# Decoder layer on one core: routing mixture on the anchors alone, adapter factor in two halves, FFN products redistributed

## The chip, the cores and the metric

The kernel runs on one core of a Trainium2 chip. The metric is the device time of one execution in microseconds. A core has TensorE (PE: matmuls, with weight loads shown apart as PEld), VectorE (DVE), ScalarE (ACT), GpSimd (POOL) and a queue engine SP that issues DMAs; each runs its own list of instructions in order and they meet only by semaphores.

## The reference, cut to what matters

One decoder layer over x of 2 sequences x 256 tokens x 512 (512 tokens in all): a Mamba-like mixer (128 heads of 64 channels), a product with a quantised context, and an FFN with a routed low-rank adapter. Only the last part is touched:

```
H = x @ W.T + b                      # 512 x 512
z = x @ A                            # rank 32
anchors = arange(1, T, 2)            # every second token, 128 of a sequence's 256
logits  = 0.5*H[anchors,:8]/max|.| + 0.5*(z[anchors] @ LiMEs.T)/max|.|
probs   = softmax(logits); weights = normalised(probs * sigmoid((probs - 2nd best)/0.5))
p_mix   = repeat(weights, 2 tokens) @ LiMEs          # 512 x 32, equal for both tokens of a pair
out     = x_before + H + ((z * p_mix) @ Bmat) * 0.5
```

## The kernel before, in words

All 512 tokens lie in one piece. Tiles of the layer's end are four token tiles t = 0..3 of 128 tokens; tiles 0 and 1 are the first sequence, 2 and 3 the second. Some 770 us go to the mixer: 64 slots (pairs of heads) in a software pipeline in which TensorE projects, scans and projects back. The change touches nothing there. Then comes a hand-written tail, in which the order of each engine's instructions is the order of the code.

The tail's last stage, the FFN, is where the change lies. `ffn(t, passes)` (L1284) issues up to three passes of the FFN product of token tile t into its own PSUM bank `work[t]` (`ps_h`, `ps_z`, `ps_y`, `ps_t` for t = 0..3): upper x upper, upper x lower, lower x upper part of numbers split in two, each pass 4 matmuls of 128x512 at line L1243. Between these passes stand TensorE's small steps for the routing, each waiting for VectorE or ScalarE:

- L1316 and L1320: turn the anchors' H and multiply the anchors' z by LiMEs.
- L1325 and L1328: the two maxima turned and spread to all partitions.
- L1334: when VectorE has the weights (`MIX_WT`, its last step is L1042), two transposes bring them to [8 experts, 256 anchors] in PSUM. ScalarE copies them to `wT` (L658).
- L1338: one plain fp32 matmul (recorded as two) makes the mixture `p_mix`, with `wT` read twice per anchor by a broadcast pattern, so that 512 columns come out.

From there the adapter's factor is made: VectorE multiplies z, the constant and the mixture to `zp` (L1048, 32x512); ScalarE rounds it to the upper part in `zst` (L661) and once more into the next 32 rows (L662); VectorE subtracts the upper part from `zp` for the lower part (L1052). `zst` (96 rows, held in tile `y_hi`) is the stationary operand of four closing matmuls, one for each token tile (L1346), which add the adapter to the four FFN banks (`d_mm`). VectorE adds bank, residual and row sum into `acc` (L1057), tile by tile, and SP stores each tile (L271).

Semaphores: `mix_dve` counts VectorE's routing steps, `mix_act` ScalarE's, `mix_pe` TensorE's; the constants `MIX_WT` and `MIX_ZP` are counts of `mix_dve`. Before the change TensorE waits once, ahead of all four closing matmuls:

```
eng.wait_ge(mix_dve, MIX_ZP + 1)
eng.wait_ge(mix_act, 5)
```

Of the kernel before, what the change touches and what calls it, by code (L numbers as in the profile page):

```python
# [6 lines left out]
B, S = 2, 256  # L7
T = B * S
P = 128
# [14 lines left out]
EXPERTS, RANK = 8, 32  # L24
# [5 lines left out]
OUT_SCALE = 16.0 / RANK  # L30
# [12 lines left out]
def build(nc, x_d, ctx_d, wdt_d, dtpar_d, normw_d, wmain_d, wbc_d, quant_d, wffn_d, ffnb_d,  # L43
# [5 lines left out]
    with ExitStack() as ctx:  # L49
# [67 lines left out]
        limes = sb("limes", [EXPERTS, RANK])  # L117
# [310 lines left out]
        def _(eng):  # L428
# [230 lines left out]

            eng.wait_ge(mix_dve, MIX_ZP)  # L660
            eng.activation(zst[0:RANK, :], zp, ACT.Copy).then_inc(mix_act, 1)  # L661
            eng.activation(zst[RANK:2 * RANK, :], zp, ACT.Copy).then_inc(mix_act, 1)  # L662


        @block.vector
        def _(eng):
# [311 lines left out]
            def mix(ins):  # L978
                n_mix[0] += 1
                ins.then_inc(mix_dve, 1)  # L980
# [42 lines left out]
            for b in range(B):  # L1023
# [23 lines left out]
            eng.wait_ge(mix_pe, 5)  # L1047
            mix(eng.scalar_tensor_tensor(out=zp, in0=zh[0:RANK, :], scalar=OUT_SCALE, in1=ps_out[0:RANK, 0, :],  # L1048
                                         op0=ALU.mult, op1=ALU.mult))
            assert n_mix[0] == MIX_ZP  # L1050
            eng.wait_ge(mix_act, 4)
            mix(eng.tensor_tensor(zst[2 * RANK:3 * RANK, :], zp, zst[0:RANK, :].bitcast(f32), ALU.subtract))  # L1052
            for t in range(TT):
# [8 lines left out]
        def _(eng):  # L1062
# [221 lines left out]
            def ffn(t, passes=(0, 1, 2)):  # L1284

                eng.wait_ge(x_add, t + 1)
                eng.wait_ge(ffn_low, 1)
                eng.wait_ge(low_wbc, GROUPS + 1)
                products(work[t][:], lambda k: wffn(k, True), lambda k: wffn(k, False), t, passes)
# [39 lines left out]
            ffn(1, (2,))  # L1329
            ffn(2, (0, 1))  # L1330

            eng.wait_ge(mix_dve, MIX_WT)
            for b in range(B):
                done = tr(ps_out[0:EXPERTS, 1, b * P:(b + 1) * P], ffn_small[:, 7, b, :])  # L1334
            done.then_inc(mix_pe, 1)
            ffn(2, (2,))
            eng.wait_ge(mix_act, 3)
            mm(ps_out[0:RANK, 0, :], limes[:], wT.unsqueeze(2).broadcast_to([EXPERTS, T // 2, 2]), start=True,  # L1338
               stop=True).then_inc(mix_pe, 1)
            ffn(3)  # L1340
            eng.wait_ge(mix_dve, MIX_ZP + 1)
            eng.wait_ge(mix_act, 5)
            eng.wait_ge(bstlo_done, 1)
            eng.wait_ge(bst_done, 2)
            for t in range(TT):
                mm(work[t][:], zst[:, t * P:(t + 1) * P], bst, start=False, stop=True,  # L1346
                   skip_group_check=True).then_inc(d_mm, 1)
# [93 lines left out]
```

## Time and profile before

| | us |
|---|---|
| median of 3 runs (lowest, highest) | 816.22 (814.41, 816.71) |
| the profiled execution's own time | 814.25 |
| its span in the trace | 812.4 |
| TensorE busy (matmul) | 787.0 |
| VectorE / ScalarE / GpSimd busy | 615.7 / 603.5 / 624.1 |
| granted TensorE clock, mean | 0.996 |

The span runs from the first to the last recorded event. Times in the trace are from the span's start. A matmul's duration includes its way through the array, so that consecutive ones overlap: what a matmul costs a stream is the distance between starts. In the grouped lines the columns are the line, engine, operation, output<-inputs, shapes and count, then busy us and mean ns of one, then the idle time before it and what ended that.

### The profile page before, as it was taken

How to read it: one execution, taken by the hardware profiler on the slowest of the kernel's cores; microseconds unless marked ns; L12 is line 12 of the kernel's file. 1: busy time of each engine (PE TensorE's matmuls, PEld its weight loads, DVE VectorE, ACT ScalarE, POOL GpSimd, SP SyncE). 2: the span in 40 equal slices, each digit the busy share in tenths (PEclk: the TensorE clock that was granted, in tenths of full speed). 3: DMA queues.
4: the chain of work that ended last, by engine and by line, in shares of the span. 5: the costliest groups of instructions: out<-in, count | busy, mean ns of one | idle time of the engine just before them, and what ended most of it. 6: DMA issues, size and time to landing. Idle time of an engine off the chain costs nothing.

```text
span 812.4 us, 13296 instructions
## 1 busy us (share of the span) xinstructions
PE 787.0 (97%) x4322; PEld 607.8 (75%) x4322; DVE 615.7 (76%) x752; ACT 603.5 (74%) x1052; POOL 624.1 (77%) x552
## 2 busy tenths in 40 slices
PE   8798999999999999999999999999999999999897
PEld 7576777777777777777777777777777777777664
DVE  6889978786776867786776867776786867798864
ACT  5788777877788776877688886878688876888442
POOL 6689985799578985799578985799578986798231
PEclk9999999999999999999999999999999999999999
DMA  8452425333243324334233424333233424340001
GB/s 332 146 142 86 130 67 177 122 118 130 92 134 123 129 65 158 127 129 129 91 129 129 129 65 156 129 129 129 91 129 129 129 66 157 130 126 30 4 2 52
DMA packets 48812, 94.93 MB, mean 117 GB/s; under 512 B 3952, under 2 KB 36848, under 8 KB 48784
## 3 DMA queue, kind: packets, MB, share of 16 engines
q1 hardware_dynamic: 48496, 94.06, 35.0%
q10 hardware_dynamic: 288, 0.52, 0.2%
q8 instruction: 15, 0.25, 0.1%
q14 instruction: 13, 0.11, 0.0%
HBM read 93.26 MB, written 1.31 MB: 116 GB/s over the span
## 4 chain that ended last, share of the span: by engine, by line
PE 58%; DVE 21%; ACT 11%; issue 8%; POOL 1%; DMA 0%; ACTq 0%; DVEq 0%
PE ps_z L1093 17%; PE ps_out L1196 14%; PE ps_h L1093 12%; PE ps_y L1183 6%; DVE conv L728 5%; DVE conv_bc L728 4%; ACT decay L531 4%; DVE yg L852 2%; PE ps_t L1066 2%; ACT L531 2%; DVE v L846 2%; ACT conv L477 2%; DVE y_lo L858 2%; DVE decay L792 1%; ACT conv_bc L461 1%
## 5 line engine op out<-in xcount | busy, mean ns | idle before, releaser
L728 DVE SCALAR_TENSOR_TENSOR conv<-ps_h,w_raw,conv 128x510 f32<-128x510 f32 (+2 forms) x192 | 143.2, 746 | 94.5 <-ACT conv L477 90.0
L531 ACT ACTIVATE decay<-csx,cs_own 128x256 f32<-128x256 f32 (+1 forms) x512 | 184.4, 443 | 1.0
L297 POOL TENSOR_TENSOR win_lo<-w_raw,win_hi 128x1024 fp32r<-128x1024 f32 x64 | 153.4, 2397 | 0.5 <-DMA csx<-cs_rows 0.5
L399 POOL TENSOR_TENSOR sqacc<-sqacc,sq 128x512 f32<-128x512 f32 x47 | 70.3, 1496 | 94.1 <-ACT sq L567 94.1
L792 DVE TENSOR_TENSOR decay<-decay,cbm 128x1536 f32<-128x1536 f32 x64 | 126.0, 1968 | 2.4 <-ACT decay L531 2.4
L539 ACT ACTIVATE hidT<-conv 128x512 f32<-128x512 f32 x64 | 40.5, 634 | 94.8 <-DVE conv L728 94.8
L1183 PE MATMUL ps_y<-decay,hid_dt 128*64 128x256 f32 (+1 forms) x1024 | 97.5, 333 | 9.4 <-DVE hid_dt L835 9.4
L337 POOL TENSOR_SCALAR_AFFINE_SELECT csx<-csx 128x512 f32<-128x512 f32 x128 | 105.8, 851 | 0.2 <-DMA csx<-cs_rows 0.2
L1183 PEld LDWEIGHTS ps_y<-decay,hid_dt 128*64 128x64 f32 x1024 | 63.4, 136 | 51.9 <-issue 17.3
L1196 PE MATMUL ps_out<-wout_hi,y_lo 128*128 128x512 f32 x252 | 99.9, 397 | 0.0
L1196 PE MATMUL ps_out<-wout_lo,y_hi 128*128 128x512 f32 x252 | 99.5, 395 | 0.0
L1196 PE MATMUL ps_out<-wout_hi,y_hi 128*128 128x512 f32 x252 | 99.4, 395 | 0.0
L302 POOL TENSOR_TENSOR wout_lo<-w_raw,wout_hi 128x512 fp32r<-128x512 f32 x64 | 94.1, 1470 | 0.1
L858 DVE SCALAR_TENSOR_TENSOR y_lo<-yg,w_raw,y_hi 128x512 fp32r<-128x512 f32 x64 | 92.7, 1448 | 1.6 <-ACT y_hi L561 1.6
L531 ACT ACT_TABLE_LOAD x63 | 80.8, 1283 | 1.2
L1093 PE MATMUL ps_z<-hT_hi,win_hi 128*128 128x512 f32 x256 | 77.1, 423 | 0.5 <-DVE conv_bc L728 0.3
L1093 PE MATMUL ps_h<-hT_hi,win_hi 128*128 128x512 f32 x256 | 73.5, 408 | 0.0
L1093 PE MATMUL ps_z<-hT_lo,win_hi 128*128 128x512 f32 x256 | 70.6, 397 | 0.0
L1093 PE MATMUL ps_h<-hT_lo,win_hi 128*128 128x512 f32 x256 | 70.2, 396 | 0.0
L1093 PE MATMUL ps_z<-hT_hi,win_lo 128*128 128x512 f32 x256 | 69.9, 394 | 0.0
L1093 PE MATMUL ps_h<-hT_hi,win_lo 128*128 128x512 f32 x256 | 69.3, 392 | 0.0
L288 POOL TENSOR_SCALAR win_hi<-w_raw 128x1024 fp32r<-128x1024 f32 x63 | 65.7, 1043 | 0.0
(316 smaller groups left out, 1483.0 us busy)
## 6 DMA issues: line engine op xcount, KB each, us to landing
w_raw<-in_wmain SPq DMA_DIRECT2D x64, 772.0 KB, 4.3
csx<-cs_rows SPq DMA_DIRECT2D x128, 256.0 KB, 3.5
bc_raw<-in_wbc SPq DMA_DIRECT2D x8, 517.0 KB, 3.5
ctx_raw<-in_ctx SPq DMA_DIRECT2D x1, 2048.0 KB, 16.4
bc_raw<-in_wffn SPq DMA_DIRECT2D x2, 512.0 KB, 4.0
out_x<-acc SPq DMA_DIRECT2D x4, 256.0 KB, 2.1
acc<-in_x ACTq DMA_DIRECT2D x2, 256.0 KB, 3.7
acc<-in_x SPq DMA_DIRECT2D x2, 256.0 KB, 3.5
```

Of the source, the lines that this page charges most:

```text
L288: eng.tensor_scalar(win_hi[:, r2, :], w_raw[:, r4, 0:W_IN], 1.0, 0.0, ALU.mult, ALU.add).then_inc(hi_win, 1)
L297: eng.tensor_tensor(win_lo[:, r2, :], w_raw[:, r4, 0:W_IN], win_hi[:, r2, :].bitcast(f32), ALU.subtract).then_inc(low_win, 1)
L302: eng.tensor_tensor(wout_lo[:, r4, :], w_raw[:, r4, W_IN:W_ALL], wout_hi[:, r4, :].bitcast(f32), ALU.subtract).then_inc(low_wout, 1)
L337: eng.affine_select(out=blocks[:, :, to:to + P], in_=blocks[:, :, at:at + P], compare_op=ALU.is_ge, fill=never, base=0, pattern=[[0, 2 * B ...
L399: eng.tensor_tensor(sqacc[:], sqacc[:], sq[:, (k - 1) % 2, :], ALU.add).then_inc(pool_sq, 1)
L531: done = eng.activation(decay[:, r2, b, h, lo:lo + n], csx[:, r2, b, h, lo:lo + n], ACT.Exp, bias=cs_own[:, r2, t, h:h + 1])
L728: eng.scalar_tensor_tensor(out=out_b[:, :, back:], in0=src_b[:, :, 0:S - back], scalar=w[:, TAPS - 1 - back:TAPS - back], in1=out_b[:, :, ...
L792: eng.tensor_tensor(decay[:, r2], decay[:, r2], cbm[:].unsqueeze(2).broadcast_to([P, B, 2, MJ]), ALU.mult).then_inc(dve_m, 1)
L858: eng.scalar_tensor_tensor(out=y_lo[:, q2, :], in0=yg[:, q2, :], scalar=w_raw[:, q4, W_ALL + 6:W_ALL + 7], in1=y_hi[:, q2, :].bitcast(f32) ...
L1093: last = mm(out, w[:, k * P:(k + 1) * P], h[:, k, :], start=n == 0, stop=n == 3 * KT - 1)
L1183: done = mm(ps_y[h * HD:(h + 1) * HD, (b + 1) * S - n:(b + 1) * S], hid_dt[:, q2, src, h * HD:(h + 1) * HD], decay[:, q2, b, h, lo:lo + n] ...
L1196: done = mm(ps_out[:, t, :], y[:, q2, t * P:(t + 1) * P], w[:, q4, :], start=pair == 0 and n == 0, stop=pair == PPG - 1 and n == 2)
```

## The change

It does five things in the layer's last stage, and nothing outside it:

1. The mixture (L1338, now L1347) is computed for the 256 anchors alone, without the doubled reading of `wT`.
2. The product with z (L1048, now L1052) is split in two halves, one for each sequence, and reads each anchor's column twice by a broadcast pattern.
3. ScalarE's two roundings and VectorE's subtraction are done once for each half: upper part and its copy for half 0, then for half 1.
4. The closing matmuls 0 and 1 wait for half 0, 2 and 3 for half 1.
5. TensorE's order: the third pass of `ffn(2)` goes ahead of the wait for the weights; the first pass of `ffn(3)` goes between the transposes and the mixture, the other two behind it.

```diff
--- before.py
+++ after.py
@@ -657,9 +657,11 @@
             eng.wait_ge(mix_pe, 4)
             eng.activation(wT, ps_out[0:EXPERTS, 1, 0:T // 2], ACT.Copy).then_inc(mix_act, 1)
 
-            eng.wait_ge(mix_dve, MIX_ZP)
-            eng.activation(zst[0:RANK, :], zp, ACT.Copy).then_inc(mix_act, 1)
-            eng.activation(zst[RANK:2 * RANK, :], zp, ACT.Copy).then_inc(mix_act, 1)
+            for b in range(B):
+                half = slice(b * S, (b + 1) * S)
+                eng.wait_ge(mix_dve, MIX_ZP + b)
+                eng.activation(zst[0:RANK, half], zp[:, half], ACT.Copy).then_inc(mix_act, 1)
+                eng.activation(zst[RANK:2 * RANK, half], zp[:, half], ACT.Copy).then_inc(mix_act, 1)
 
 
         @block.vector
@@ -1045,11 +1047,18 @@
             eng.wait_ge(bst_done, 1)
             eng.tensor_tensor(bst[RANK:2 * RANK, :], bmat, bst[0:RANK, :].bitcast(f32), ALU.subtract).then_inc(bstlo_done, 1)
             eng.wait_ge(mix_pe, 5)
-            mix(eng.scalar_tensor_tensor(out=zp, in0=zh[0:RANK, :], scalar=OUT_SCALE, in1=ps_out[0:RANK, 0, :],
-                                         op0=ALU.mult, op1=ALU.mult))
-            assert n_mix[0] == MIX_ZP
-            eng.wait_ge(mix_act, 4)
-            mix(eng.tensor_tensor(zst[2 * RANK:3 * RANK, :], zp, zst[0:RANK, :].bitcast(f32), ALU.subtract))
+            for b in range(B):
+                half = slice(b * S, (b + 1) * S)
+                mix(eng.scalar_tensor_tensor(out=zp[:, half].rearrange("r (a two) -> r a two", two=2),
+                                             in0=zh[0:RANK, half].rearrange("r (a two) -> r a two", two=2),
+                                             scalar=OUT_SCALE,
+                                             in1=ps_out[0:RANK, 0, b * P:(b + 1) * P].unsqueeze(2)
+                                             .broadcast_to([RANK, P, 2]), op0=ALU.mult, op1=ALU.mult))
+            assert n_mix[0] == MIX_ZP + 1
+            for b in range(B):
+                half = slice(b * S, (b + 1) * S)
+                eng.wait_ge(mix_act, 4 + 2 * b)
+                mix(eng.tensor_tensor(zst[2 * RANK:3 * RANK, half], zp[:, half], zst[0:RANK, half].bitcast(f32), ALU.subtract))
             for t in range(TT):
                 eng.wait_ge(d_mm, t + 1)
                 eng.wait_ge(bias_add, t + 1)
@@ -1327,22 +1336,21 @@
             eng.wait_ge(mix_dve, MIX_SCALES)
             mm(ps_out[:, 3, D // 2:D // 2 + 2], onesf[:], ffn_one[0:2, 4, 0:2], start=True, stop=True).then_inc(mix_pe, 1)
             ffn(1, (2,))
-            ffn(2, (0, 1))
+            ffn(2)
 
             eng.wait_ge(mix_dve, MIX_WT)
             for b in range(B):
                 done = tr(ps_out[0:EXPERTS, 1, b * P:(b + 1) * P], ffn_small[:, 7, b, :])
             done.then_inc(mix_pe, 1)
-            ffn(2, (2,))
+            ffn(3, (0,))
             eng.wait_ge(mix_act, 3)
-            mm(ps_out[0:RANK, 0, :], limes[:], wT.unsqueeze(2).broadcast_to([EXPERTS, T // 2, 2]), start=True,
-               stop=True).then_inc(mix_pe, 1)
-            ffn(3)
-            eng.wait_ge(mix_dve, MIX_ZP + 1)
-            eng.wait_ge(mix_act, 5)
+            mm(ps_out[0:RANK, 0, 0:T // 2], limes[:], wT, start=True, stop=True).then_inc(mix_pe, 1)
+            ffn(3, (1, 2))
             eng.wait_ge(bstlo_done, 1)
             eng.wait_ge(bst_done, 2)
             for t in range(TT):
+                eng.wait_ge(mix_dve, MIX_ZP + 2 + t // 2)
+                eng.wait_ge(mix_act, 5 + 2 * (t // 2))
                 mm(work[t][:], zst[:, t * P:(t + 1) * P], bst, start=False, stop=True,
                    skip_group_check=True).then_inc(d_mm, 1)
```

TensorE, from the FFN product of token tile 2 to that of tile 3 (names: `wout_hi` and `wout_lo` hold the turned x, `ffn_small` the weights, `conv_bc` is `wT`). Before:

```order
L1243 MATMUL ps_y<-wffn_lo,wout_hi 128x512 x2
L1066 MATMUL ps_out<-ident,ffn_small 8x128 [waits mix_dve]
L1066 MATMUL ps_out<-ident,ffn_small 8x128
L1243 MATMUL ps_y<-wbc_hi,wout_lo 128x512 [waits low_wbc,ffn_low,x_add]
L1243 MATMUL ps_y<-wbc_hi,wout_lo 128x512
L1243 MATMUL ps_y<-wffn_hi,wout_lo 128x512 x2
L1338 MATMUL ps_out<-conv_bc,limes 32x512 [waits mix_act]
L1243 MATMUL ps_t<-wbc_hi,wout_hi 128x512 [waits low_wbc,ffn_low,x_add]
L1243 MATMUL ps_t<-wbc_hi,wout_hi 128x512
L1243 MATMUL ps_t<-wffn_hi,wout_hi 128x512 x2
L1243 MATMUL ps_t<-wbc_lo,wout_hi 128x512 x2
L1243 MATMUL ps_t<-wffn_lo,wout_hi 128x512 x2
```

Now:

```order
L1252 MATMUL ps_y<-wbc_hi,wout_lo 128x512 x2
L1252 MATMUL ps_y<-wffn_hi,wout_lo 128x512 x2
L1075 MATMUL ps_out<-ident,ffn_small 8x128 [waits mix_dve]
L1075 MATMUL ps_out<-ident,ffn_small 8x128
L1252 MATMUL ps_t<-wbc_hi,wout_hi 128x512 [waits low_wbc,ffn_low,x_add]
L1252 MATMUL ps_t<-wbc_hi,wout_hi 128x512
L1252 MATMUL ps_t<-wffn_hi,wout_hi 128x512 x2
L1347 MATMUL ps_out<-conv_bc,limes 32x256 [waits mix_act]
L1252 MATMUL ps_t<-wbc_lo,wout_hi 128x512 [waits low_wbc,ffn_low,x_add]
L1252 MATMUL ps_t<-wbc_lo,wout_hi 128x512
L1252 MATMUL ps_t<-wffn_lo,wout_hi 128x512 x2
L1252 MATMUL ps_t<-wbc_hi,wout_lo 128x512 x2
```

The third pass of tile 2 has moved from behind the transposes to ahead of them; the first pass of tile 3 took its place; the mixture matmul is 256 wide, with two passes of tile 3 behind it instead of three.

VectorE, its last rows (`conv` is `zp`, `v` holds z, `y_hi` is `zst`). Before:

```order
L1042 TENSOR_TENSOR ffn_small<-ffn_small,ffn_one 128x16 [waits mix_dve]
L1046 TENSOR_TENSOR y_lo<-sqacc,y_lo 32x512 [waits bst_done]
L1048 SCALAR_TENSOR_TENSOR conv<-v,ps_out 32x512 [waits mix_pe]
L1052 TENSOR_TENSOR y_hi<-conv,y_hi 32x512 [waits mix_act]
L1057 SCALAR_TENSOR_TENSOR acc<-acc,rowsum,ps_h 128x512 [waits r_sum,bias_add,d_mm]
L1057 SCALAR_TENSOR_TENSOR acc<-acc,rowsum,ps_z 128x512 [waits r_sum,bias_add,d_mm]
L1057 SCALAR_TENSOR_TENSOR acc<-acc,rowsum,ps_y 128x512 [waits r_sum,bias_add,d_mm]
L1057 SCALAR_TENSOR_TENSOR acc<-acc,rowsum,ps_t 128x512 [waits r_sum,bias_add,d_mm]
```

Now:

```order
L1048 TENSOR_TENSOR y_lo<-sqacc,y_lo 32x512 [waits bst_done]
L1052 SCALAR_TENSOR_TENSOR conv<-v,ps_out 32x256 [waits mix_pe]
L1052 SCALAR_TENSOR_TENSOR conv<-v,ps_out 32x256
L1061 TENSOR_TENSOR y_hi<-conv,y_hi 32x256 [waits mix_act] x2
L1066 SCALAR_TENSOR_TENSOR acc<-acc,rowsum,ps_h 128x512 [waits r_sum,bias_add,d_mm]
L1066 SCALAR_TENSOR_TENSOR acc<-acc,rowsum,ps_z 128x512 [waits r_sum,bias_add,d_mm]
L1066 SCALAR_TENSOR_TENSOR acc<-acc,rowsum,ps_y 128x512 [waits r_sum,bias_add,d_mm]
L1066 SCALAR_TENSOR_TENSOR acc<-acc,rowsum,ps_t 128x512 [waits r_sum,bias_add,d_mm]
```

One multiplication became two of half the width, and so did the subtraction; both subtractions stand ahead of the first closing addition.

ScalarE, its last rows. Before:

```order
L653 ACTIVATE ffn_small<-ffn_small 128x16 [waits mix_dve]
L655 ACTIVATE ffn_small<-ffn_small 128x16 [waits mix_dve]
L658 ACTIVATE conv_bc<-ps_out 8x256 [waits mix_pe]
L661 ACTIVATE y_hi<-conv 32x512 [waits mix_dve]
L662 ACTIVATE y_hi<-conv 32x512
```

Now:

```order
L655 ACTIVATE ffn_small<-ffn_small 128x16 [waits mix_dve]
L658 ACTIVATE conv_bc<-ps_out 8x256 [waits mix_pe]
L663 ACTIVATE y_hi<-conv 32x256 [waits mix_dve]
L664 ACTIVATE y_hi<-conv 32x256
L663 ACTIVATE y_hi<-conv 32x256 [waits mix_dve]
L664 ACTIVATE y_hi<-conv 32x256
```

Two 512-wide roundings became four of 256, with a wait for each half. The lists of GpSimd and SP are unchanged.

## Rows read from the trace of the kernel before

**Rows 1.** The page: busy us of each engine, share, instructions.
```profile
PE 787.0 (97%) x4322; PEld 607.8 (75%) x4322; DVE 615.7 (76%) x752; ACT 603.5 (74%) x1052; POOL 624.1 (77%) x552
```

**Rows 2.** Chain of waits, end of the program: start us, us, what.
```profile
801.34 0.18 DVE ffn_small L1042
...
801.57 0.38 PE ps_out L1066 x2
801.95 0.92 PE ps_y L1243 x4
802.88 0.97 PE ps_out L1338 x2
803.85 2.97 PE ps_t L1243 x12
```

**Rows 3.** Stretches of the end: us, busy of PE, PEld, DVE, ACT, POOL, then PEclk.
```profile
800.60:801.57 0.97, 0.01 (x1) 0.00 (x1) 0.80 (x6) 0.00 (x0) 0.00 (x0) 1.00 0.00 0
801.57:807.77 6.20, 6.18 (x24) 3.83 (x24) 2.70 (x5) 1.64 (x3) 0.00 (x0) 1.00 0.00 0
```

**Rows 4.** TensorE in order of time, 799.9 to 804: start us, us, what.
```profile
799.99 0.62 PE L1243 MATMUL ps_y<-wffn_lo,wout_hi 128*128 128x512 f32 x2
...
802.26 0.61 PE L1243 MATMUL ps_y<-wffn_hi,wout_lo 128*128 128x512 f32 x2
802.81 1.04 PE L1338 MATMUL ps_out<-conv_bc,limes 8*32 8x512 f32 x2
```

**Rows 5.** All engines in order of time, 803.7 to the end.
```profile
803.78 0.30 PEld L1243 LDWEIGHTS ps_t<-wbc_hi,wout_hi 128*128 128x128 f32 x2 [0.84 <-issue]
...
803.88 0.68 DVE L1048 SCALAR_TENSOR_TENSOR conv<-v,ps_out 32x512 f32<-32x512 f32 x1 [1.66 <-PE ps_out L1338]
...
804.59 0.63 ACT L661 ACTIVATE y_hi<-conv 32x512 fp32r<-32x512 f32 x1 [2.23 <-DVE conv L1048]
...
805.25 0.63 ACT L662 ACTIVATE y_hi<-conv 32x512 fp32r<-32x512 f32 x1
805.26 0.68 DVE L1052 TENSOR_TENSOR y_hi<-conv,y_hi 32x512 fp32r<-32x512 f32 x1 [0.70 <-ACT y_hi L661]
...
806.43 0.19 PEld L1346 LDWEIGHTS ps_h<-y_lo,y_hi 96*128 96x128 f32 x1
806.65 0.39 PE L1346 MATMUL ps_h<-y_lo,y_hi 96*128 96x512 f32 x1
...
807.09 0.75 DVE L1057 SCALAR_TENSOR_TENSOR acc<-acc,rowsum,ps_h 128x512 f32<-128x512 f32 x1 [1.15 <-PE ps_h L1346]
...
809.07 0.74 DVE L1057 SCALAR_TENSOR_TENSOR acc<-acc,rowsum,ps_t 128x512 f32<-128x512 f32 x1
```

**Rows 6.** TensorE, groups by shape, 793 to the end: plain fp32 products.
```profile
L1338 PE MATMUL ps_out<-conv_bc,limes 8*32 8x512 f32 x2 | 1.0, 600 | 0.0
...
L1066 PE MATMUL ps_out<-ident,ffn_small 128*8 128x128 f32 x2 | 0.4, 273 | 1.0 <-DVE ffn_small L1042 1.0
```

**Rows 7.** ScalarE, groups by shape, whole span.
```profile
L531 ACT ACTIVATE decay<-csx,cs_own 128x256 f32<-128x256 f32 x256 | 127.6, 498 | 1.0
...
L658 ACT ACTIVATE conv_bc<-ps_out 8x256 f32<-8x256 f32 x1 | 0.4, 374 | 2.0 <-PE ps_out L1066 2.0
...
L655 ACT ACTIVATE ffn_small<-ffn_small 128x16 f32<-128x16 f32 x1 | 0.2, 215 | 1.1 <-DVE ffn_small L1026 1.1
```

**Rows 8.** VectorE, groups by shape, 793 to the end.
```profile
L1048 DVE SCALAR_TENSOR_TENSOR conv<-v,ps_out 32x512 f32<-32x512 f32 x1 | 0.7, 676 | 1.7 <-PE ps_out L1338 1.7
...
L1020 DVE TENSOR_TENSOR ffn_small<-ffn_small,ffn_one 128x16 f32<-128x16 f32 x1 | 0.2, 176 | 0.0
...
L1034 DVE TENSOR_TENSOR ffn_small<-ffn_small 128x16 f32<-128x16 f32 x1 | 0.2, 174 | 0.0
```

**Rows 9.** Stretches early in the mixer, columns as in Rows 3.
```profile
30.00:35.00 5.00, 3.94 (x20) 2.87 (x18) 2.47 (x14) 4.94 (x12) 1.56 (x5) 1.00 0.30 102
35.00:40.00 5.00, 2.86 (x19) 2.07 (x20) 4.88 (x6) 4.98 (x11) 4.49 (x4) 0.84 0.41 130
```

## The prediction

> **What bounds the kernel now.** I first read the page's busy times. TensorE works 787.0 of 812.4 us [rows 1], but that share is an average over the mixer, which the change leaves alone. All that it touches lies in the last 12 us, so the question is which wait ends last there. The chain of waits answers that [rows 2]: VectorE's last routing step (L1042) ends at 801.52, the two transposes start at 801.57, then come 0.92 us for four FFN matmuls of token tile 2, 0.97 us for the mixture matmul, and 2.97 us for the twelve FFN matmuls of tile 3. From 801.57 on the end is a sum of TensorE's work. Ahead of it TensorE stands still: from 800.60 to 801.57 it is busy for 0.01 us, while VectorE computes [rows 3]. So the reader is to see two things: a hole of 0.97 us with ready work behind it, and behind the hole a stream with no hole.
>
> The third view is the order in time from 803.7 [rows 5]. The adapter's factor takes VectorE and ScalarE from 803.88 to 805.94 (multiply, upper part, lower part), while TensorE is busy with tile 3 until it loads the closing weights at 806.43. That path has 0.49 us to spare. VectorE's first closing addition starts at 807.09, 0.44 us behind the start of the first closing matmul (806.65); the four additions run 0.66 us apart ((809.07 - 807.09) / 3), the last ends at 809.81, and a store lands the span's end at 812.4. The matmuls behind them come 0.23 us apart, so the additions set the pace there, and the end moves with the first addition.
>
> **The change, part by part.** All is counted in the profiled execution: span 812.40, own time 814.25. The median of the runs shown is 816.22, 2.0 us above it, so the saving is taken off the median at the end.
>
> *The hole.* The third pass of tile 2 goes ahead of the wait. The last two FFN matmuls before the hole start at 799.99 and 800.22: two in 0.62 us, each 0.39 long, 0.23 apart [rows 4]. Four more start by 801.14 and end at 801.53. The wait is released at 801.52 and the transposes began at 801.57 [rows 2]. Must they now wait for TensorE? The nearest row of a small plain product behind such matmuls is the mixture: the two ahead of it end at 802.87 and it starts at 802.81 [rows 4], 0.06 us earlier. By that the transposes could start at 801.47, so VectorE still sets their start: 0 us lost. The bounds are 0 and 0.1 us. Between transposes and mixture stand four matmuls as before, of tile 3 now. The mixture's other condition, ScalarE's copy to `wT` (0.37 us [rows 7], begun when the transposes end at 801.95 [rows 2]), is done by 802.4, and the mixture starts at 802.81 as before. What this saves lies behind: of twelve matmuls of tile 3, eight are left after the mixture. Four times 0.23 is **0.92 us**.
>
> *The mixture.* It is recorded as two matmuls of 600 ns [rows 6] in 1.04 us [rows 4], hence 0.44 us apart. At 128 columns the same kind takes 273 ns each [rows 6], two in 0.38 us [rows 2], so 0.11 apart. Between the two, 256 columns give 0.22 apart and about 0.38 each: 0.60 in all, ending at 803.41 instead of 803.85, **0.44 us**. Bounds: no saving if the length did not matter, which these two rows exclude, and 0.5.
>
> *TensorE's waits.* `ffn(3)` is now called twice and `ffn(2)` once, so as many waits as before. Three closing matmuls get waits of their own. No row prices a fulfilled wait; between nothing and the 0.2 us of a whole matmul each, they hide under the additions 0.66 us apart: 0.
>
> *TensorE's clock of the end.* By these, tile 3's second pass starts 0.07 us ahead of the mixture's end, as before (803.78 [rows 5]), at 803.34. From there to the first closing matmul it took 2.87 us (806.65), now 2.87 - 0.92 = 1.95: weights wanted at 805.07, matmul at 805.29, first addition at **805.73** instead of 807.09. That is 1.36 us.
>
> *The factor in halves: the cover that shrinks.* With eight matmuls behind the mixture instead of twelve, the unsplit path would no longer be hidden: mixture 803.41, multiply 0.68 to 804.12, upper part 0.63 to 804.78, subtract 0.68 to 805.49 [rows 5], each 0.03 behind the other. The closing weights would come 0.45 us later than wanted (805.52 against 805.07), and 0.91 us would be left of the gain. Split, each half costs more than half. ScalarE takes 215 ns for 16 columns [rows 7] and 630 for 512 [rows 5], so 0.42 for 256. VectorE takes 174 for 16 and 676 for 512 [rows 8], also 0.42. The broadcast reading costs nothing that a row shows: 176 ns with it (L1020), 174 without (L1034) [rows 8]. Then:
> - half 0: multiply 803.44 to 803.86, upper part 803.89 to 804.31, its copy 804.34 to 804.76, subtraction 804.34 to 804.76. The first closing weights are wanted at 805.07: 0.3 us to spare.
> - half 1: multiplied meanwhile; upper part 804.79 to 805.21, copy 805.24 to 805.66, subtraction 805.24 to 805.66.
> - closing matmul 2 wants its weights at 805.53 and gets them at about 805.69. It ends near 806.3; VectorE wants it at 805.73 + 2 x 0.66 = 807.05. Hidden.
> - the second subtraction stands in VectorE's list ahead of the first addition, and waits there for ScalarE's third rounding. It ends at 805.66, the addition starts at 805.73. This is the thinnest cover, 0.07 us, and what is late next.
>
> The bounds of a half rounding: 0.37 us (8x256 out of PSUM) and 0.50 (L531, 128x256 from SBUF with a bias column [rows 7]); at 0.50 the second subtraction ends at 805.90 and the first addition starts 0.20 us later. I take 0.42, since its ends are roundings and copies from SBUF without such a column. At the far end a half costs as much as a whole: multiply to 804.12, three roundings of 0.63 to 806.10, subtraction to 806.81, addition at 806.84; 0.25 us are left of the gain.
>
> A rule speaks against the split. The Trainium skill, VectorE: DVE Perf Modes, section The TRN2 errata, says that ScalarE and VectorE pay a fixed latency per instruction, and advises pieces of 512 elements or more. The 16-wide rows (0.215 and 0.174 us) agree on the fixed part. By its advice, the unsplit version above, the gain would be 0.91 us, by the rows split it is 1.36.
>
> The Trainium skill, ScalarE: Activation LUTs, section Rules for kernel authors, budgets about 0.3 us an ACTIVATE and 0.83 ns an element. By that a half takes an estimated 0.51 us, the addition starts 0.24 us late, and the gain would be 1.12 us. The row for 512 columns is 0.63, below that page's 0.72.
>
> **Sum:** 0.92 + 0.44 = 1.36 us, nothing lost. Own time 814.25 - 1.36 = 812.9; median 816.22 - 1.36, about 814.8, that is 0.17% less.
>
> **The rivals.**
> - *VectorE's list binds.* The second subtraction holds up the first addition, since halves cost more than the lines between 16 and 512 columns say. For it: a cover of 0.07 us. Against it: both slopes rest on the very instructions or their kind. The gain falls to 1.16 (halves at 0.50) or to 0.25 (halves at a whole's price): a median of 815.1 to 816.0. Chance 0.15; it can't turn the sign.
> - *The change doesn't do what it says:* the pass fills the hole, but TensorE gets to the transposes late, by up to 0.1 us. A median of 814.9; this lies in the forecast's own range.
> - *TensorE's clock falls, and it is slower.* The granted clock is 1.00 of the 2.4 GHz in both stretches about the hole [rows 3]. Early in the mixer it fell: in 35 to 40 us it is 0.84 on average, with TensorE busy for 2.86 of 5 us, behind 3.94 of 5 in the stretch before [rows 9]. If another order of the end brought the 1.2 GHz level from 801.57 on, the 3.72 us of TensorE's work to 805.29 would double: 3.7 - 1.36 = 2.3 us slower, a median of 818.6. It decides from 1.4 us of work at the lower level. Against it: 0.97 us without work fall away, TensorE is busier than before. Chance 0.03. The Trainium skill, TensorE: Matmul & The Clock Gate, section HAM oscillation, says that idle gaps bring the clock down; by it a filled hole is in the clock's favour.
>
> **How the numbers follow.** Forecast (gain 1.25 to 1.4) 0.82, VectorE's list 0.15, clock 0.03. A measurement tells about 0.3%, 2.4 us, from no change. The forecast gives 1.4, so "same" is the likeliest verdict although I expect a real gain. The runs of before lie 2.3 us apart (814.41 to 816.71), and their scatter can add the missing 1.0 to the gain: some 0.14 for faster. Slower: the clock, and scatter against it, 0.04. The rest, 0.82, is within. The range: from the lowest run less the largest gain with both upper bounds, 814.41 - 1.5 = 812.9, to the highest run less the smallest gain, 816.71 - 0.25, about 816.5.
>
> **What would show it.** In the trace of the changed kernel TensorE has no idle stretch ahead of the transposes (now some 0.05 us), and they start within 0.1 us of 801.57. The mixture's two matmuls span about 0.60 us. Eight FFN matmuls stand between it and the first closing one. ScalarE's last four take 0.42 each, VectorE's halves too. The first closing addition starts near 805.7, and what ends its wait is the closing matmul; if it starts right at the end of the second subtraction, VectorE's list binds and the first rival holds. The span is near 811.0. I am wrong if the span falls by less than 1.0 us with the mixer unchanged, or if the granted clock of the last stretch is below 1.00.

## The result, and the profile after

| | before | changed |
|---|---|---|
| median of 12 runs, us | 816.55 | 813.51 |
| lowest, highest | 814.38, 817.66 | 812.96, 816.20 |
| ratio, 95% interval | | 0.9972 (0.9961 to 0.9983) |
| profiled execution: own time, span | 814.25, 812.4 | 816.20, 814.3 |
| its mean granted clock | 0.996 | 0.991 |

The kernel is faster by 0.28%, 2.3 us by the ratio; the medians themselves lie 3.0 us apart. The forecast was 1.36 us, 0.17%, a ratio of 0.9983, which is the upper end of the interval. A gain of 0.28% is still under the 0.3% that the prediction took as what a measurement can tell, so its likeliest verdict, "same", came out. Yet the span of the profiled execution is longer than before's. So the first view to read is where those 1.9 us came from: the stretches of the changed kernel, columns as in [rows 3] (PEclk is the third number from the right).

```profile
10.00:12.50 2.50, 2.50 (x15) 2.50 (x16) 2.43 (x3) 1.86 (x4) 2.50 (x3) 0.61 1.01 415
12.50:15.00 2.50, 2.21 (x9) 1.47 (x8) 1.86 (x4) 2.48 (x5) 2.50 (x2) 0.71 0.93 377
35.00:40.00 5.00, 2.54 (x15) 1.54 (x15) 4.26 (x5) 4.96 (x13) 3.42 (x4) 0.79 0.32 108
80.00:90.00 10.00, 8.06 (x38) 6.07 (x39) 9.76 (x10) 6.64 (x13) 10.00 (x9) 0.83 0.41 132
775.00:780.00 5.00, 5.00 (x32) 2.55 (x30) 2.36 (x7) 2.09 (x5) 0.64 (x2) 0.66 0.00 0
785.00:800.00 15.00, 14.04 (x128) 10.73 (x126) 8.82 (x20) 6.62 (x14) 6.72 (x6) 1.00 0.01 2
```

The granted clock falls in the mixer's start, at 35 to 45 us, again at 80 to 90 us, and in the stage just ahead of the FFN. The trace of before shows only the second of these four, at 35 to 45 us [rows 9]. All of them lie ahead of anything that the change touches; from 785 us on the clock is 1.00 in both. The last stage must therefore be compared from an event of its own, not from the span's start. I take the start of the two transposes behind the routing (801.57 in [rows 2]). The chain of waits of the changed kernel, its end:

```profile
804.87 0.04 issue
804.90 0.38 PE ps_out L1075 x2
805.29 0.93 PE ps_t L1252 x4
806.21 0.55 PE ps_out L1347 x2
806.76 2.03 PE ps_t L1252 x8
```

Against [rows 2]: the transposes start 0.04 us behind what stands ahead of them in the chain, about as before, four matmuls of tile 3 (0.93 us) stand where tile 2's stood, the mixture takes 0.55 instead of 0.97, and 2.03 us of tile 3 are left instead of 2.97. The chain puts the stretch ahead of the transposes down to TensorE now, and no longer to VectorE. In order of time, TensorE's matmuls of the last stage and what stands beside them:

```profile
803.79 0.62 PE L1252 MATMUL ps_y<-wbc_hi,wout_lo 128*128 128x512 f32 x2
...
804.25 0.62 PE L1252 MATMUL ps_y<-wffn_hi,wout_lo 128*128 128x512 f32 x2
...
804.67 0.17 DVE L1044 TENSOR_TENSOR ffn_small<-ffn_small,ffn_one 128x16 f32<-128x16 f32 x1
...
804.90 0.38 PE L1075 MATMUL ps_out<-ident,ffn_small 128*8 128x128 f32 x2
...
806.14 0.61 PE L1347 MATMUL ps_out<-conv_bc,limes 8*32 8x256 f32 x2
...
806.79 0.74 DVE L1052 SCALAR_TENSOR_TENSOR conv<-v,ps_out 32x256 f32<-32x256 f32 x2 [1.23 <-PE ps_out L1347]
...
807.24 0.42 ACT L663 ACTIVATE y_hi<-conv 32x256 fp32r<-32x256 f32 x1 [1.54 <-DVE conv L1052]
...
807.69 0.42 DVE L1061 TENSOR_TENSOR y_hi<-conv,y_hi 32x256 fp32r<-32x256 f32 x1 [0.15 <-ACT y_hi L663]
...
808.12 0.42 ACT L663 ACTIVATE y_hi<-conv 32x256 fp32r<-32x256 f32 x1
...
808.57 0.42 DVE L1061 TENSOR_TENSOR y_hi<-conv,y_hi 32x256 fp32r<-32x256 f32 x1 [0.47 <-ACT y_hi L663]
808.62 0.39 PE L1354 MATMUL ps_h<-y_lo,y_hi 96*128 96x512 f32 x1
...
809.06 0.75 DVE L1066 SCALAR_TENSOR_TENSOR acc<-acc,rowsum,ps_h 128x512 f32<-128x512 f32 x1
...
811.04 0.74 DVE L1066 SCALAR_TENSOR_TENSOR acc<-acc,rowsum,ps_t 128x512 f32<-128x512 f32 x1
```

Two things are to be seen here. The last matmul of tile 2 ends at 804.25 + 0.62 = 804.87, VectorE's last routing step at 804.84, and the transposes start at 804.90: the hole is closed. TensorE's end comes 0.03 us behind VectorE's, but the transposes start 0.06 us behind VectorE, where before it was 0.05, so nothing that counts is lost. And the second half's subtraction ends at 808.99, where the first closing addition starts at 809.06. From the transposes to the first addition it is now 4.16 us, and 5.52 before (801.57 to 807.09): **1.36 us less, as forecast to the hundredth**. To the start of the last addition, the measure M of all runs below, it is 6.14 against 7.50.

### The profile page after: what moved, and what is told of

It reads as the page before. It is cut to its first block, busy times and chain, and to the rows that moved or that the text cites. A ratio compares the mean times of both kernels' runs of the same rounds, so it can differ in the third digit from the quotient of the medians.

```text
span 814.3 us, 13303 instructions
## 1 busy us (share of the span) xinstructions
PE 790.6 (97%) x4322; PEld 610.4 (75%) x4322; DVE 618.0 (76%) x754; ACT 604.3 (74%) x1054; POOL 624.6 (77%) x552
## 4 chain that ended last, share of the span: by engine, by line
PE 60%; DVE 19%; ACT 11%; issue 8%; POOL 1%; DMA 0%; DVEq 0%; ACTq 0%
PE ps_z L1102 18%; PE ps_out L1205 14%; PE ps_h L1102 12%; PE ps_y L1192 7%; DVE conv L730 4%; DVE conv_bc L730 4%; ACT decay L531 4%; PE ps_t L1075 2%; DVE yg L854 2%; ACT L531 2%; DVE v L848 2%; ACT conv L477 2%; DVE y_lo L860 1%; DVE decay L794 1%; ACT conv_bc L461 1%
## 5 line engine op out<-in xcount | busy, mean ns | idle before, releaser
L531 ACT ACTIVATE decay<-csx,cs_own 128x256 f32<-128x256 f32 (+1 forms) x512 | 184.4, 443 | 1.0
L1192 PE MATMUL ps_y<-decay,hid_dt 128*64 128x256 f32 (+1 forms) x1024 | 99.7, 338 | 9.7 <-DVE hid_dt L837 9.6
```

Source lines behind the costliest of these rows:

```text
L531: done = eng.activation(decay[:, r2, b, h, lo:lo + n], csx[:, r2, b, h, lo:lo + n], ACT.Exp, bias=cs_own[:, r2, t, h:h + 1])
L1192: done = mm(ps_y[h * HD:(h + 1) * HD, (b + 1) * S - n:(b + 1) * S], hid_dt[:, q2, src, h * HD:(h + 1) * HD], decay[:, q2, b, h, lo:lo + n] ...
```

## The experiments

Two questions were open: what each part gives, and why the timed runs show more than 1.36 us. M is read from each kernel's trace. In the runs, "full clock" is an execution with a mean granted clock of 0.999 or 1.000; in the traces at 0.999 the only stretch below 1.00 is behind the last matmul, at the span's end.

| kernel | M, us | median of 12 | ratio, interval |
|---|---|---|---|
| changed, timed again | 6.14 | 813.31 | 0.9979 (0.9966 to 0.9992) |
| changed, third time | 6.16 | 814.77 | 0.9981 (0.9967 to 0.9995) |
| before, as its own control | 7.47 | 816.46 | 1.0003 (0.9991 to 1.0015) |
| order alone | 6.93 | 815.22 | 0.9991 (0.9979 to 1.0004) |
| anchors alone | 7.05 | 816.09 | 0.9997 (0.9985 to 1.0009) |
| order and anchors, unsplit | 6.52 | 815.37 | 0.9985 (0.9973 to 0.9997) |
| halves alone | 7.50 | 817.44 | 1.0000 (0.9986 to 1.0015) |
| changed, one more rounding | 6.39 | 813.46 (one run) | |
| early closing | 5.69 | 814.44 | 0.9972 (0.9957 to 0.9986) |
| and GpSimd's subtraction | 5.64 | 813.30 | 0.9966 (0.9954 to 0.9979) |
| and closings in pairs (10 runs) | 5.63 | 813.90 | 0.9970 (0.9957 to 0.9983) |

**1. The changed kernel, again.** No edit.

> The changed kernel once more, timed anew beside the kernel before. Measure M, in this and the next runs: from the start of the two transposes behind the routing to the start of the last closing addition (7.50 us before, 6.14 in the changed kernel). Theory T (the change saves the 1.36 us of M and nothing else; the rest of the 2.3 us that the timed runs showed is scatter of the granted clock in the mixer): M 6.1 to 6.2; executions with a mean granted clock of 0.999 or 1.000 lie near 813.0 us here and near 814.4 in the kernel before, and ratios of medians wander about 0.998. Rival R (the change also alters the mixer or its clock, about 1 us more): the ratio stays near 0.997, and executions at equal granted clock differ by more than 1.8 us.

M 6.14, and the executions at full clock have a median of 812.87 (six of 12, 812.80 to 813.37), where before's nine of 35 beside it lie at 814.08 to 814.83 (median 814.33). Those are theory T's numbers, and 1.5 us between them is less than rival R's 1.8. The interval of the ratio 0.9979 holds both 0.9983 and 0.997. The two medians lie 3.2 us apart, about as in the first timing, which is more than theory T said of medians.

**2. TensorE's order alone.**

```diff
-            ffn(2, (0, 1))
+            ffn(2)
...
-            ffn(2, (2,))
+            ffn(3, (0,))
             eng.wait_ge(mix_act, 3)
...
-            ffn(3)
+            ffn(3, (1, 2))
```

> TensorE's new order alone: third pass of tile 2 ahead of the wait, first of tile 3 ahead of the mixture; mixture 512 wide, factor unsplit. Theory T: four matmuls less behind the mixture (0.92 us), but the factor ends 4.37 us behind the transposes' start as before, where the closing weights are wanted at 3.94, so about half is lost: M 7.04, gain 0.46 us, and VectorE's subtraction ends the wait of the first closing weights. Rival U (the factor is not binding even unsplit): M 6.6, gain 0.9.

M 6.93: a gain of 0.57 of the possible 0.92. The rest is the unsplit factor, as the order of time shows:

```profile
803.94 0.68 DVE L1048 SCALAR_TENSOR_TENSOR conv<-v,ps_out 32x512 f32<-32x512 f32 x1 [1.65 <-PE ps_out L1338]
...
804.65 0.63 ACT L661 ACTIVATE y_hi<-conv 32x512 fp32r<-32x512 f32 x1 [2.22 <-DVE conv L1048]
...
805.31 0.68 DVE L1052 TENSOR_TENSOR y_hi<-conv,y_hi 32x512 fp32r<-32x512 f32 x1 [0.70 <-ACT y_hi L661]
805.34 0.63 PE L1243 MATMUL ps_t<-wffn_hi,wout_lo 128*128 128x512 f32 x2
...
806.05 0.50 PE L1346 MATMUL ps_h<-y_lo,y_hi 96*128 96x512 f32 x1
...
806.59 0.75 DVE L1057 SCALAR_TENSOR_TENSOR acc<-acc,rowsum,ps_h 128x512 f32<-128x512 f32 x1 [0.59 <-PE ps_h L1346]
```

TensorE's last FFN matmul ends at 805.97; the subtraction ends at 805.99 and only then can the closing weights be loaded, so the first closing matmul starts at 806.05, 0.71 us behind the start of the last FFN pair, where it was 0.45 behind it in the changed kernel (808.17 to 808.62). Rival U falls.

**3. The anchors alone.**

```diff
-            mm(ps_out[0:RANK, 0, :], limes[:], wT.unsqueeze(2).broadcast_to([EXPERTS, T // 2, 2]), start=True,
-               stop=True).then_inc(mix_pe, 1)
+            mm(ps_out[0:RANK, 0, 0:T // 2], limes[:], wT, start=True, stop=True).then_inc(mix_pe, 1)
...
-            mix(eng.scalar_tensor_tensor(out=zp, in0=zh[0:RANK, :], scalar=OUT_SCALE, in1=ps_out[0:RANK, 0, :],
-                                         op0=ALU.mult, op1=ALU.mult))
+            mix(eng.scalar_tensor_tensor(out=zp.rearrange("r (a two) -> r a two", two=2),
+                                         in0=zh[0:RANK, :].rearrange("r (a two) -> r a two", two=2),
+                                         scalar=OUT_SCALE,
+                                         in1=ps_out[0:RANK, 0, 0:T // 2].unsqueeze(2)
+                                         .broadcast_to([RANK, T // 2, 2]), op0=ALU.mult, op1=ALU.mult))
```

> Mixture on the 256 anchors alone, broadcast in the product with z, all else as before and unsplit. Theory T: mixture 0.60 us instead of 1.04, the product with z still 0.68, factor hidden: M 7.06, gain 0.44. Rival: the broadcast reading costs VectorE up to twice, 1.2 us for the product; the factor then ends about 0.03 us late, so the product's own duration tells, not M.

M 7.05, a gain of 0.45. The broadcast reading is free, against the rival; VectorE's groups by shape show the product at the same 676 ns as in [rows 8]:

```profile
L1048 DVE SCALAR_TENSOR_TENSOR conv<-v,ps_out 32x512 f32<-32x512 f32 x1 | 0.7, 676 | 1.2 <-PE ps_out L1341 1.2
```

Its span was 815.6, the longest of all traces, though the mixer ran at full clock. The stretches say why:

```profile
200.00:760.00 560.00, 555.75 (x2961) 431.29 (x2962) 423.54 (x472) 429.86 (x750) 449.18 (x393) 1.00 0.35 115
770.00:775.00 5.00, 3.80 (x34) 2.73 (x34) 4.24 (x14) 3.94 (x6) 1.38 (x3) 0.75 0.01 3
775.00:780.00 5.00, 5.00 (x31) 2.93 (x30) 1.78 (x4) 0.88 (x3) 0.22 (x1) 0.57 0.00 0
...
785.00:800.00 15.00, 14.04 (x133) 10.82 (x131) 8.81 (x18) 6.23 (x14) 6.72 (x6) 1.00 0.00 1
800.00:810.00 10.00, 9.00 (x40) 6.23 (x39) 5.66 (x23) 2.64 (x6) 0.00 (x0) 1.00 0.01 2
```

The clock fell in the stage of the context product alone, whose code is the same in all kernels.

**4. Order and anchors without the halves** (edits of 2 and 3 together).

> The changed kernel without the halves: one product with z, one rounding with its copy, one subtraction. Theory T: the factor ends 3.93 us behind the transposes' start, wanted at 3.50: M 6.60, gain 0.90 over before, 0.46 slower than the changed kernel. Rival (a fixed cost for each instruction eats what the halves give): M 6.2 or less.

M 6.52: the halves are worth 0.38 us here. The rival, that the fixed cost for each instruction eats them, falls.

**5. The halves alone**: the changed kernel with the order and the 512-wide mixture of before, whose columns the product reads once each.

```diff
-                                             in1=ps_out[0:RANK, 0, b * P:(b + 1) * P].unsqueeze(2)
-                                             .broadcast_to([RANK, P, 2]), op0=ALU.mult, op1=ALU.mult))
+                                             in1=ps_out[0:RANK, 0, half].rearrange("r (a two) -> r a two", two=2),
+                                             op0=ALU.mult, op1=ALU.mult))
...
-            ffn(2)
+            ffn(2, (0, 1))
...
-            ffn(3, (0,))
+            ffn(2, (2,))
...
-            mm(ps_out[0:RANK, 0, 0:T // 2], limes[:], wT, start=True, stop=True).then_inc(mix_pe, 1)
-            ffn(3, (1, 2))
+            mm(ps_out[0:RANK, 0, :], limes[:], wT.unsqueeze(2).broadcast_to([EXPERTS, T // 2, 2]), start=True,
+               stop=True).then_inc(mix_pe, 1)
+            ffn(3)
```

> The halves alone: TensorE's order and the 512-wide mixture of before. The whole factor was hidden before, so theory T says no gain: M 7.50, ratio 1.000 within the scatter. It is also the control for the rival R (any edit, or its place in the timed series, shifts the mixer by some us): R would have it 0.997 or so, with M 7.50.

M 7.50, ratio 1.0000: no gain, and no shift of the mixer by an edit as such, against rival R in that form. The parts alone give 0.57 + 0.45 + 0.00 = 1.02 us, all of them 1.36: the halves give nothing by themselves and 0.38 once the other two have taken their cover away.

**6. One more rounding between the halves.**

```diff
                 eng.activation(zst[0:RANK, half], zp[:, half], ACT.Copy).then_inc(mix_act, 1)
+                if b == 0:
+                    eng.activation(spare_half[:], zp[:, half], ACT.Copy)
                 eng.activation(zst[RANK:2 * RANK, half], zp[:, half], ACT.Copy).then_inc(mix_act, 1)
```

> The changed kernel with one more rounding of 256 columns on ScalarE, to a spare tile, between the halves. It tests whether the second subtraction stands within 0.1 us of holding up the first closing addition. Theory T: the second subtraction ends 0.45 us later, the first closing addition starts 0.40 us later, right at its end: M 6.54. Rival (the closing matmuls alone set the additions, with cover left): M 6.14 to 6.3.

M 6.39, 0.25 over the changed kernel; between the two numbers given. The order of time settles it:

```profile
804.21 0.42 ACT L664 ACTIVATE y_hi<-conv 32x256 fp32r<-32x256 f32 x1 [1.54 <-DVE conv L1055]
...
804.54 0.40 ACT L666 ACTIVATE spare_half<-conv 32x256 f32<-32x256 f32 x1
...
804.95 0.42 ACT L667 ACTIVATE y_hi<-conv 32x256 fp32r<-32x256 f32 x1
...
805.39 0.42 ACT L664 ACTIVATE y_hi<-conv 32x256 fp32r<-32x256 f32 x1
...
805.60 0.40 PE L1357 MATMUL ps_h<-y_lo,y_hi 96*128 96x512 f32 x1
...
805.84 0.42 DVE L1064 TENSOR_TENSOR y_hi<-conv,y_hi 32x256 fp32r<-32x256 f32 x1 [0.76 <-ACT y_hi L664]
...
806.29 0.75 DVE L1069 SCALAR_TENSOR_TENSOR acc<-acc,rowsum,ps_h 128x512 f32<-128x512 f32 x1
```

The first closing matmul ended at 806.00, but the first addition started at 806.29, 0.03 behind the end of the second subtraction: VectorE's list binds, as theory T had it. The size was off because the added rounding, 0.40 long, moved the second half's by 0.29 and not 0.45: it started 0.33 behind the rounding ahead of it, while that was still running. The second half's starts 3.51 us behind the transposes here (801.88) and 3.22 in the changed kernel (808.12 less 804.90). Since a waiting addition starts 0.03 behind the subtraction's end, only 0.04 of the 0.07 us between the two in the changed kernel is cover; 0.29 less 0.04 is the 0.25 measured.

**7. A version to beat both: early closing.** The closing matmuls 0 and 1 need nothing of tile 3, and the mixture waits for its place behind four matmuls although ScalarE's `wT` is ready some 0.45 us before (in the changed kernel at 805.69, against 806.14). `piece(t, lo, hi)` issues matmuls lo to hi of a tile's twelve; `close(t)` is the closing matmul with its waits.

```diff
-            ffn(3, (0,))
+            piece(3, 0, 2)
...
-            ffn(3, (1, 2))
+            piece(3, 2, 8)
...
+            close(0)
+            piece(3, 8, 10)
+            close(1)
+            piece(3, 10, 12)
+            close(2)
+            close(3)
```

> A version meant to beat both: only two matmuls of tile 3 ahead of the mixture, closing matmul 0 after eight of tile 3's twelve, closing 1 after ten. Theory T: factor 0.46 us earlier; first addition follows the second subtraction at 3.78 us behind the transposes' start: M 5.76, 0.38 under the changed kernel. Rival: switching TensorE between the two kinds of product costs more than it gives, M 6.1 or more.

```profile
807.19 0.42 DVE L1061 TENSOR_TENSOR y_hi<-conv,y_hi 32x256 fp32r<-32x256 f32 x1 [0.46 <-ACT y_hi L663]
...
807.64 0.75 DVE L1066 SCALAR_TENSOR_TENSOR acc<-acc,rowsum,ps_h 128x512 f32<-128x512 f32 x1
```

M 5.69, against 5.76 expected: 0.45 under the changed kernel. The first addition starts 3.71 us behind the transposes (803.93 here) and 0.03 behind the second subtraction's end, as theory T said; the rival's M of 6.1 did not come.

**8. And GpSimd's subtraction.** VectorE's subtraction of half 1 is taken out, and GpSimd does it behind its last bias addition.

```diff
+            eng.wait_ge(bias_add, TT)
+            eng.wait_ge(mix_dve, MIX_ZP + 2)
+            eng.wait_ge(mix_act, 6)
+            eng.tensor_tensor(zst[2 * RANK:3 * RANK, S:T], zp[:, S:T], zst[0:RANK, S:T].bitcast(f32),
+                              ALU.subtract).then_inc(mix_dve, 1)
```

> The same with the second half's subtraction on GpSimd (some 0.7 to 0.8 us there), so that nothing stands ahead of the first closing addition on VectorE but the first half. Theory T: first addition at 3.54, M 5.52, 0.6 under the changed kernel. Rival: GpSimd needs over 1.2 us, closing matmul 2 comes late, and M is 5.8 or more.

```profile
805.01 0.47 PE L1315 MATMUL ps_h<-y_lo,y_hi 96*128 96x512 f32 x1
...
805.32 0.63 PE L1308 MATMUL ps_t<-wbc_hi,wout_lo 128*128 128x512 f32 x2
805.36 0.73 POOL L428 TENSOR_TENSOR y_hi<-conv,y_hi 32x256 fp32r<-32x256 f32 x1 [10.74 <-ACT y_hi L668]
805.52 0.75 DVE L1069 SCALAR_TENSOR_TENSOR acc<-acc,rowsum,ps_h 128x512 f32<-128x512 f32 x1 [0.77 <-PE ps_h L1315]
...
805.79 0.40 PE L1315 MATMUL ps_z<-y_lo,y_hi 96*128 96x512 f32 x1
...
806.03 0.63 PE L1308 MATMUL ps_t<-wffn_hi,wout_lo 128*128 128x512 f32 x2
806.23 0.75 DVE L1069 SCALAR_TENSOR_TENSOR acc<-acc,rowsum,ps_z 128x512 f32<-128x512 f32 x1
...
806.49 0.39 PE L1315 MATMUL ps_y<-y_lo,y_hi 96*128 96x512 f32 x1
...
806.92 0.75 DVE L1069 SCALAR_TENSOR_TENSOR acc<-acc,rowsum,ps_y 128x512 f32<-128x512 f32 x1
807.59 0.74 DVE L1069 SCALAR_TENSOR_TENSOR acc<-acc,rowsum,ps_t 128x512 f32<-128x512 f32 x1
```

The first addition starts 3.57 us behind the transposes (801.95 here), as expected, and GpSimd takes 0.73. But M is 5.64, not 5.52: closing matmul 2 starts at 806.49 and ends at 806.88, and the third addition follows at 806.92, 1.40 behind the first, where two steps of VectorE's pace of 0.66 make 1.32. GpSimd's subtraction ended at 806.09, well ahead of that, so the rival falls too. What is late next is TensorE.

**9. Closings in pairs**: `close(0)`, `close(1)`, then `piece(3, 8, 12)`.

> The version with GpSimd's subtraction, but closing matmuls 0 and 1 together after eight of tile 3's twelve, and 2 and 3 after the rest: TensorE changes once less between kinds of product. Theory T: that change cost some 0.1 us there and held closing matmul 2 back; M 5.5, against 5.64. Rival: the additions are set by the first one and their own pace, M 5.6 or more.

M 5.63. The first two additions stand 0.67 apart, but closing matmul 2 now ends at 809.37 + 0.39 = 809.76, the third addition starts at 809.81, 1.40 behind the first again. So the rival's number came out, though for TensorE's reason, and theory T's 0.1 us of changing kinds is not what held it back: the closing matmul 2 starts 4.53 us behind the transposes here (804.84) and 4.54 in version 8, behind the same twelve matmuls of tile 3. At full clock this version ran at 812.02 and 812.03. The intervals of versions 7 to 9 all lie below 1. Against the changed kernel the timed runs do not separate them, only the traces do (0.5 us): at full clock version 7's three runs lie at 812.85 to 813.00, no better than the changed kernel's 812.99 below, although its M is 0.45 less.

**10. The controls of the scatter.** Before against itself, and the changed kernel a third time.

> The kernel before against itself, as the control of the comparison. Theory T (the gain beyond 1.4 us is scatter of the granted clock ahead of the last stage): 12 runs, of which a quarter to a third at a clock of 0.999, near 814.4 us; the rest 816 to 818; ratio 0.999 to 1.001, and M 7.50. Rival R': the share of executions at full clock is a property of the kernel, a third here and a half in the changed kernel, and this control repeats the third.

> The changed kernel a third time, in the same call as the control, for the share of executions at full clock. Theory T: near 813.0 us at 0.999 or above, M 6.14, ratio 0.997 to 0.999; share at full clock as in the control within what 12 runs can tell. Rival R': again half or more at full clock.

The control gave 1.0003, with two of 12 at full clock (814.22, 814.41), fewer than either theory had said. The third timing gave 0.9981, five of 12 at full clock; twelve runs each cannot tell five from two. Pooled over the timings of the experiments, and for the changed kernel the first timing too:

| | runs | at full clock | their median | their range | median of the rest |
|---|---|---|---|---|---|
| before (three timings and the control) | 103 | 24 | 814.40 | 814.05 to 814.97 | 816.70 |
| changed (three timings) | 36 | 17 | 812.99 | 812.66 to 814.30 | 815.19 |

At full clock the two kernels differ by 1.41 us, beside 1.36 in the traces. This group is not quite even: nine of the changed kernel's 17 show 1.000 and none of before's; at 0.999 alone the difference is 1.17 (813.23 against 814.40). What goes beyond it is how often an execution gets the full clock: 17 of 36 against 24 of 103. Chance alone would split them so unevenly about once in 100 (an exact test of the two shares), yet the other kernels in which TensorE's hole is closed had 15 of 58, and those in which it is open (anchors alone, halves alone) 2 of 24. In all thirteen traces the falls lie ahead of 785 us, in instructions that do not differ.

One figure seems to speak for rival R: at equal mean clocks below 0.999 the kernels lie further apart than 1.8 us (at 0.996, seven runs of before have a median of 816.27 and three of the changed kernel 813.94; at 0.998, eleven have 815.97 and two 813.19). But the mean does not say where the clock fell, and the place decides the price. The trace of before has one fall, at 35 to 45 us, and its span of 812.4 us is that of the control without one (812.3). The third timing of the changed kernel has one fall of about the same size, in the stage of the context product, and its span is 812.6 where the second timing without a fall has 811.2:

```profile
770.00:775.00 5.00, 3.80 (x31) 1.93 (x29) 3.66 (x13) 3.35 (x6) 1.32 (x2) 0.84 0.01 2
775.00:780.00 5.00, 5.00 (x44) 3.16 (x43) 2.55 (x6) 2.06 (x4) 0.55 (x1) 0.82 0.00 0
```

Whether the change has a hand in how often and where the clock falls stays open.

## Why the prediction was right

- **What bounds the end** was read right: from VectorE's last routing step on, the end is a sum of TensorE's work. With the factor split, both terms moved the end by their own size; without the split the new order alone gave 0.57 of its 0.92 us.
- **The hole, 0.92 us.** The four matmuls fit (804.87 against VectorE's end at 804.84), the transposes lost nothing, the stream behind the mixture shrank by 0.94. The 0 that was taken out of the bounds 0 to 0.1 held.
- **The mixture, 0.44.** It took 0.61 against 0.60 forecast, and alone gave 0.45.
- **TensorE's added waits, 0.** Closing matmul 2 got its weights late, starting 0.27 instead of 0.23 behind matmul 1, and the additions kept 0.66 apart. Hidden, as said.
- **The halves.** 0.42 us for ScalarE's and 0.42 for VectorE's subtraction, 0.40 for its product, against 0.42 forecast for all. The first addition started 0.07 us behind the second subtraction's end, as forecast. Only 0.04 of that is cover, and experiment 6 showed that VectorE's list binds once it is used up. The 16-column end of the prediction's line for ScalarE (L655) is an exponential and not a copy; the halves still came out at its 0.42. Without the split 0.45 was to be lost; 0.38 was. The step that was a little off is the start of a closing matmul behind a wait. I let it follow its weights by 0.22 as in the stream, but with TensorE idle it started 0.06 behind the subtraction's end (experiment 2) and then took 0.50 instead of 0.39. That is 0.1 us earlier in all.
- **The page that speaks against small pieces** (the Trainium skill, VectorE: DVE Perf Modes, section The TRN2 errata) is right about the fixed part, 0.42 is more than half of 0.63; its advice would have cost 0.38 us here. The page's budget for ScalarE (the Trainium skill, ScalarE: Activation LUTs, section Rules for kernel authors), 0.51 us for a half, was too high by 0.09: the Trainium skill gives it there for an activation whose bias is a column operand, and these have none. The row that has one (L531, 0.50 us in [rows 7]) agrees with it.
- **The rivals.** VectorE's list binding did not come about, by 0.04 us. The clock did fall, but not in the last stage: from 785 us to the last matmul it is 1.00 in all thirteen traces, in the four with the hole and in the nine without. Nor did it fall more often than before (19 of the changed kernel's 36 runs are below full clock, 79 of before's 103).
- **The number.** 814.8 was forecast and 813.5 measured, within the range, but only 0.6 us above its lower end; the gain is 2.3 us by the ratio and 3.0 by the medians, and not 1.4. The mechanism's size was right (1.36 in the trace, 1.41 between executions at full clock). The step that fell short is "the saving is taken off the median": before's median is that of executions with clock losses, 2 us above its full-clock time, and the medians of 12 carry how many such executions each kernel got. In the two later timings the medians lie 3.2 and 1.6 us apart, and the ratios are 0.9979 and 0.9981, nearer to the forecast's 0.9983. So the 1.36 us are understood and shown; that the median also fell within the range owes something to a range as wide as the scatter.

## What to carry to other kernels

A hole in the critical engine is worth what can be put into it, but only together with the path that was hidden behind that work: price the filling, then ask what now ends last, and shorten that in the same change. Measure a change of a few tenths of a per cent from an event of its own inside the trace; span and median carry clock losses from elsewhere that are larger than the change. A split that gives nothing by itself can be worth something (here 0.38 us) once the work that hid the unsplit path is gone.

## What the runs showed of the hardware

- The granted clock falls in some executions of a kernel and not in others, always at some of the same few places (10 to 15, 35 to 45, 80 to 90 and 770 to 780 us). TensorE is not fully busy there (in the changed kernel's trace without falls, 4.3 of 5 us from 10, 2.7 of 5 from 35, 9.1 of 10 from 80 and 3.8 of 5 from 770), but the first 10 us, with 7.1 of 10, never showed one.
- The mean clock tells an execution's time only roughly: 814.05 to 814.97 us for all 24 of before at 0.999, 816.9 to 817.7 for those at 0.990, but 815.9 to 818.4 at 0.996, and 814.25 for the profiled execution, which is at 0.996 too. What a fall costs depends on where it lies: about nothing at 35 to 45 us, 1.4 us at 770 to 780 (experiment 10).
- An extra ScalarE rounding of 256 columns put between two others moved its successor by 0.29 us although it lasts 0.40; consecutive roundings elsewhere start 0.44 apart. It signals no semaphore and writes another tile than the others; which of these let it start early is not shown. The duration of a row is not always what it costs.
- A broadcast operand from PSUM, each column read twice, costs VectorE nothing in a product of 512 columns: 676 ns with and without (experiment 3), and in halves of 256 columns 404 ns with (changed) and without (experiment 5).
